# Second layer unrolled with a closer expert order; blank rows and expert weights placed in the first layer

## The reference

```python
x = x + ln(attention_16_heads(ln(x)) + ln(x))          # first layer, heads of 8 features, 256 tokens each
x = x + ln(ffn(ln(x)))                                 # second layer

def ffn(x):
    y = ln(x + mha(x)) * g1 + be1                      # 4 heads of 32, attention over the 16 sequences
    logits = y @ Wg.T                                  # 8 experts
    e = argmax(logits)                                 # one expert for each of the 4,096 tokens
    moe = relu(y @ W1[e] + b1[e]) @ W2[e] + b2[e]      # 128 -> 512 -> 128
    return ln(y + moe) * g2 + be2
```

## Time and profile before

| what | value |
|---|---|
| median of 3 runs | 700.91 us (698.33 to 701.24) |
| the profiled execution, its own time | 701.92 us |
| its span, first to last instruction | 700.2 us |
| TensorE's mean granted clock | 0.922 |
| busy share PE, DVE, ACT, POOL | 83%, 61%, 54%, 44% |
| first layer | 0 to about 376.5 us |
| second attention with the sort | about 376.5 to 574 us |
| experts | about 575 to 700 us |

### The profile page before, as it was taken

One profiled execution on the slowest core, in us unless ns is written; L12 is line 12 of the kernel. 1 busy time (PEld: TensorE's weight loads), 2 busy tenths in 40 slices (PEclk: granted clock), 3 DMA queues, 4 the chain that ended last, 5 costly groups with the idle time before them and its releaser, 6 DMA issues. The chain is left out here.

```text
span 700.2 us, 16679 instructions
## 1 busy us (share of the span) xinstructions
PE 581.0 (83%) x5511; PEld 432.2 (62%) x5511; DVE 428.4 (61%) x1210; ACT 377.7 (54%) x991; POOL 305.5 (44%) x535
## 2 busy tenths in 40 slices
PE   4999999999999999999972888888878109999920
PEld 3655666666666666666641787777765109999910
DVE  2454666666666666666523578888885603788870
ACT  1014665565666655655560698878851004677760
POOL 5321133233332332322134537777767720077676
PEclk9999999999999999999995799999978558999975
DMA  5000000000000000000015500000001112144333
GB/s 152 13 2 2 4 1 18 17 7 13 17 18 17 18 18 18 7 12 18 17 33 169 140 2 1 1 2 0 0 22 43 56 57 66 34 59 61 34 32 32
DMA packets 28593, 21.60 MB, mean 31 GB/s; under 512 B 3514, under 2 KB 26850, under 8 KB 28515
## 3 DMA queue, kind: packets, MB, share of 16 engines
q1 hardware_dynamic: 21186, 15.29, 8.7%
q0 software_dynamic: 6640, 4.92, 5.1%
q10 hardware_dynamic: 688, 0.39, 0.2%
HBM read 10.11 MB, written 8.12 MB: 26 GB/s over the span
## 5 line engine op out<-in xcount | busy, mean ns | idle before, releaser
L383 DVE TENSOR_REDUCE nmax<-psA 128x2 f32<-128x512 f32 x256 | 165.1, 687 | 121.5 <-PE psA L206 121.2
L511 ACT ACTIVATE pr<-psB 128x512 f32<-128x512 f32 x250 | 135.8, 595 | 123.4 <-PE psB L223 122.7
L206 PE MATMUL psA<-km,q 24*128 24x256 f32 x768 | 139.8, 428 | 3.4 <-POOL km L606 2.1
L223 PE MATMUL psB<-q,km 26*128 26x256 f32 (+1 forms) x752 | 109.9, 411 | 0.0
L206 PEld LDWEIGHTS psA<-km,q 24*128 24x128 f32 x768 | 91.7, 198 | 29.3 <-issue 17.5
L1620 POOL DMA_INDIRECT out<-wz,ys x39 | 61.1, 1568 | 60.7 <-ACT wz L1585 54.3
L606 POOL TENSOR_TENSOR km<-kraw,rows_of 128x768 f32<-128x768 f32 x16 | 23.5, 1467 | 118.6 <-DVEq L362 114.6
L237 PE MATMUL psO<-pr,v 128*32 128x256 f32 x1024 | 69.4, 389 | 1.3 <-ACT osb L505 1.1
L223 PEld LDWEIGHTS psB<-q,km 26*128 26x128 f32 (+1 forms) x752 | 69.0, 189 | 0.2 <-issue 0.2
L580 POOL TENSOR_SCALAR ve<-mv_r 128x2 f32<-128x2 f32 x16 | 3.7, 232 | 123.5 <-DVE mv_r L344 123.5
L1489 DVE TENSOR_TENSOR hT<-psH,e_nb1T 128x512 f32<-128x512 f32 x39 | 27.0, 692 | 42.4 <-PE psH L1450 33.0
(11 more groups left out here) (203 smaller groups left out, 1224.0 us busy)
## 6 DMA issues: line engine op xcount, KB each, us to landing
ys<-y_sorted SPq DMA_DIRECT2D x39, 72.0 KB, 1.8
xs<-x_all SPq DMA_DIRECT2D x16, 128.0 KB
e_w<-W SPq DMA_DIRECT2D x1, 2048.0 KB
e_w<-W SPq DMA_DIRECT2D x4, 512.0 KB
out<-x_all SPq DMA_DIRECT2D x15, 128.0 KB, 3.7
x_all<-x SPq DMA_DIRECT2D x1, 1536.0 KB, 10.0
q<-mT SPq DMA_DIRECT2D x64, 4.0 KB
out<-wz,ys POOLq DMA_INDIRECT x39
```

The source lines that it names most:

```text
L206: last = T.matmul(psA[:, n % 2, c * L1:(c + 1) * L1], queries(b, h, depth, slice(c * P, (c + 1) * P)), keys(b, h, depth, slice(0, L1)), st ...
L223: last = T.matmul(bank_of(b, h)[:, c * L1:(c + 1) * L1], keys(b, h, depth, slice(c * P, (c + 1) * P)), queries(b, h, depth, slice(0, L1)), ...
L383: V.tensor_reduce(nmax[:, b % 2, :, h], psA[:, n % 2, :].rearrange("p (c m) -> p c m", c=2), AX.X, ALU.max, negate=True).then_inc(S["a_fre ...
L511: A.activation(pr[:, h % PRING, :, :].rearrange("p c l -> p (c l)"), bank_of(b, h), ACT.Exp, scale=SCALE1).then_inc(S["b_free"], 1)
```

## The change

Weights and blank rows: the nine loads of expert parameters move from SP at the start of the second block to ScalarE's queue in iterations 1 to 5 of the first layer, two per iteration. GpSimd makes the blank rows in iteration 1 of the first layer, and ScalarE writes them over the whole region of each expert, one region at the start of each of the iterations 6 to 13, and over the region of the spare blocks in iteration 14. SP's fills after the sort are gone, as is the cast of the row numbers for them. `send` waits for the nine fills.

```diff
+            def fill(e):
+                act.wait_ge(S["blank_ok"], 1)
+                lo, hi = e * REGION, (e + 1) * REGION if e < NE else LAST_ROW
+                rows = blank[:, e:e + 1, :].broadcast_to([P, NT + 1, YROW]) if e < NE else blank[:, NE:, :]
+                act.dma_start(y_sorted[lo:hi, :].rearrange("(m p) d -> p m d", p=P), rows).then_inc(blanked, 16)
...
             for i in range(LAST + 3):
+                if 1 <= i <= 5:
+                    for to, source in loads[2 * i - 2:2 * i]:
+                        act.dma_start(to, source, allow_slow_non_contiguous=True).then_inc(loaded, 16)
+                if 6 <= i <= 6 + NE:
+                    fill(i - 6)
                 iteration(i)
...
-            for to, source in loads:
-                sp.dma_start(to, source, allow_slow_non_contiguous=True).then_inc(loaded, 16)
...
-            for e in range(NE):
-                r = sp.value_load(pad_i[0:1, e:e + 1], min_val=0, max_val=LAST_ROW - P)
-                sp.dma_start(y_sorted[bass.ds(r, P), :], zeros[:, e, :]).then_inc(S["padded"], 16)
```

```diff
-SORT_AT = {16: 0, 17: 1, 20: 2}
-BIAS_AT = 19
-SEND_AT = {17: (0, 0), 18: (0, 4), 19: (1, 0), 20: (1, 4), 21: (2, 0), 22: (2, 4)}
+CHUNKS = ((0, 8), (8, 8), (16, 8), (24, 4), (28, 4))
+SORT_AT = {12: 0, 16: 1, 20: 2, 22: 3}
+SEND_AT = {13: (0, 0, 2), 14: (0, 2, 2), 15: (0, 4, 2), 16: (0, 6, 2), 17: (1, 0, 2), 18: (1, 2, 2), 19: (1, 4, 2),
+           20: (1, 6, 2), 21: (2, 0, 2), 22: (2, 2, 6), 23: (3, 0, 4)}
...
+            def late_scales(i, n):
+                dve.wait_ge(S["yln_step"], 3 * i)
+                dve.wait_ge(S["sd_ok"], i - SETS + 1)
+                V.reciprocal(rs_y[:, :], sd_y[:, :]).then_inc(S["late_step"], 1)
+                dve.wait_ge(S["late_step"], i - SETS + 1)
+                V.scalar_tensor_tensor(out=nb_y[:, :], in0=mv_y[:, n, :, 0], scalar=-1.0, in1=rs_y[:, :],
+                                       op0=ALU.mult, op1=ALU.mult).then_inc(S["yln_step"], 1)
...
+            def late_norm(i, n):
+                act.wait_ge(S["yagg"], i + 1)
+                act.wait_ge(S["consts"], 2)
+                act.wait_ge(S["late_step"], i - SETS)
+                A.activation(sd_y[:, :], mv_y[:, n, :, 1], ACT.Sqrt, bias=eps[:, :]).then_inc(S["sd_ok"], 1)
+                act.wait_ge(S["yln_step"], 3 * i + 1)
+                for c in range(2):
+                    last = A.activation(yn[:, c, :], r2[:, n, c, :], ACT.Identity, bias=nb_y[:, c:c + 1],
+                                        scale=rs_y[:, c:c + 1])
+                last.then_inc(S["yln_step"], 1)
```

```diff
+                if (g := at(t, 4)) is not None:
+                    first_norm(g)
+                if (g := at(t, 9)) is not None:
+                    second_norm(g, range(0, min(2, SIZES[g])))
+                if (g := at(t, 10)) is not None:
+                    second_norm(g, range(2, SIZES[g]))
...
-            for t in range(STEPS):
-                for g, k in members(t, 11):
-                    put(FIRST[g] + k)
+            for t in range(NS):
+                put(t)
```

More of the change, by code:

```diff
@@ L29, in count, with first_layer @@
     return max(value, 0) if isinstance(value, int) else value
-def first_layer(nc, x, w_qkv, b_qkv, w_o, b_o, ident, identh, minus_half, xs, out, kept, loads2, loaded2):
+def first_layer(nc, x, w_qkv, b_qkv, w_o, b_o, ident, identh, minus_half, xs, out, kept, loads2, loaded2, loads,
+                loaded, blank, y_sorted, blanked):
     with ExitStack() as ctx:
@@ L644, in _ @@
                 iteration(i)
+                if i == 1:
+                    blank_rows()
         @block.sync
@@ L813, in pipeline, with run @@
         def pipeline(iteration):
[L816 to L822, removed]
+            def run():
+                for t in range(NSTEP + 8):
                     iteration(t, t % 4)
@@ L826, in late, with rooted @@
         def late(t):
-            return isinstance(t, int) and t >= NSTEP
+            return t >= NSTEP
+        def rooted(t):
+            return t >= NSTEP + 2
         block = ctx.enter_context(nc.Block())
@@ L903, in iteration @@
                     pe.wait_ge(S["lg_ok"], count(t - 8))
+                    pe.wait_ge(S["sums_read"], sum(at < t for at in SORT_AT))
+                    if t in SORT_AT:
+                        sums(SORT_AT[t])
                     if has(t, 4):
@@ L1016, in find @@
             def find(k):
-                n = SORT_STEPS * k + 4
+                first, n = CHUNKS[k]
                 dve.wait_ge(S["sums_full"], k + 1)
-                V.tensor_copy(run[0][:, Z:, :].rearrange("p j e -> p (j e)"),
-                              psQK[:, CHUNK * NE:2 * CHUNK * NE]).then_inc(S["sorting"], 1)
-                dve.wait_ge(S["sorting"], n + 1)
-                for step in range(3):
+                sort_step(V.tensor_copy(run[0][:, Z:Z + n, :].rearrange("p j e -> p (j e)"),
+                                        psAL[:, SUMS + n * NE:SUMS + 2 * n * NE]))
@@ L1024, in find @@
+                steps = n.bit_length() - 1
+                for step in range(steps):
                     a, b = run[step % 2], run[1 - step % 2]
-                    V.tensor_tensor(b[:, Z:, :], a[:, Z:, :], a[:, Z - 2 ** step:Z + CHUNK - 2 ** step, :],
-                                    ALU.add).then_inc(S["sorting"], 1)
-                    dve.wait_ge(S["sorting"], n + 2 + step)
-                V.tensor_tensor(place[:, :, :], psQK[:, 0:CHUNK * NE].rearrange("p (j e) -> p j e", e=NE),
-                                run[1][:, Z - 1:Z - 1 + CHUNK, :], ALU.add).then_inc(S["sorting"], 1)
@@ L1088, in iteration @@
                     V.tensor_copy(y_all[:, bass.ds(i * 2, 2), 0:P], yout[:, n, :, :]).then_inc(S["y_kept"], 1)
-                if late(t) and has(t, 6):
-                    finish_y(t - 6, m % 2, t)
+                if rooted(t) and has(t, 6):
+                    late_scales(t - 6, m % 2)
                 if has(t, 5):
@@ L1107, in iteration @@
                     last.then_inc(S["yagg"], 1)
+                if late(t) and has(t, 6):
+                    finish_y(t - 6, m % 2, t)
                 if has(t, 8):
@@ L1318, in iteration @@
                     last.then_inc(S["start_ok"], 1)
-                if has(t, 6):
+                if has(t, 6) and not rooted(t):
                     i, n = t - 6, m % 2
@@ L1423, in at @@
             return None
-        def members(t, lag):
-            turns = [(g, t - (ends(g) - 1 + lag)) for g in range(GROUPS)]
-            return [(g, k) for g, k in turns if 0 <= k < SIZES[g]]
-        STEPS = NS + 14
+        STEPS = NS + 11
         block = ctx.enter_context(nc.Block())
```

248 lines of the change are left out of this document (123 added, 125 removed).

## The result

The changed kernel took a median of 702.59 us (699.62 to 706.53 in undisturbed executions), the kernel before 701.17 in as many executions beside it: a ratio of 1.0036, with a 95% interval of 1.0019 to 1.0054. The loss of 0.36% is clear of zero by its interval, but it is less than the 0.5% that was named ahead of time as the bound of a change. Forecast were 690.1, a gain, and a range of 679 to 701. The profiled execution took 701.88 us and spans 700.1, so its parts can be set directly against the 700.2 of the profile before.

The account below looks back on a forecast made before the run. TensorE was taken to bound the first layer and the expert tiles, with waits for GpSimd, SyncE's blank-row stores and outstanding adds elsewhere. Terms -0.8 + 3.6 + 4.5 + 4.1 - 7.0 - 11.4 - 3.8 = -10.8 gave 690.1 us, range 679 to 701.

Parts of the forecast that it names:

- The fills in the first layer: First layer: weight loads and blank-row fills issued by ScalarE cost nothing; SyncE's small loads beside them bounded at 0 to 1 us per iteration.
- The rival that a fill's issue holds ScalarE: First layer: each of eight large fills blocks ScalarE 3.6 to 7.9 us, 30.8 us in all, total 720.9; chance 0.13.
- The closing stretch: From last logits to first expert load: 13.8 us against 25.2, ended last by the bias product; -11.4 us.
- 64 products 8.9: After the last logits: TensorE's 64 products of the expert biases take 8.9 us.
- GpSimd's last 16 stores ... end about the same time: After the last logits: GpSimd's stores from the end of step 20 finish about when the bias product does.
- The bias product at the low clock: Rival, after the last logits: product begun at 1.2 GHz takes up to twice 8.9 us; total 698, chance 0.05.
- Steps 16 to 23: Late second layer: normalisation in steps 18 to 21 on ScalarE and VectorE removes 9.9 us of waits for GpSimd; net -7.0 us.
- Sorting and stores in steps 12 to 15: Second layer: sorting adds 3.6 us at step 12; two indirect stores per step add 4.5 us in steps 14 and 15.
- TensorE's clock: Second layer: a late step opens a gap that drops TensorE's clock for one step; +4.1 us, bounds 0 and four steps.
- The rival of a fall in every sorting step: Second layer: each of steps 13 to 16 runs at 1.2 GHz, 16.4 us; total 697.9, chance 0.17.
- The loop unrolled: Second layer: the first step of the loop's second pass loses its extra time; -0.8 us.
- The experts: Expert part: two fewer indirect adds outstanding when TensorE stops, at 1.89 us each; -3.8 us, bounds 0 and -5.7.

Follow-up runs that it names:

- the later fills: Changed kernel with each of the nine fills issued some 7 us into its iteration instead of at its start; median 694.87 us, ratio 0.9944 to the kernel before.
- the paced kernel: Changed kernel with the later fills, GpSimd issuing a store only when the store two places before has landed; median 691.36 us, ratio 0.9869 to the kernel before.
- the kernel before with pacing: Kernel before the change, GpSimd issuing a store only when the store two places before has landed; median 698.3 us, ratio 0.9962.
- that part alone: Kernel before the change with only its expert part replaced by that of the changed kernel; median 696.74 us, ratio 0.9963.

## Why the prediction was wrong

- **The fills in the first layer: 0 forecast, +4.8 measured (+6.4 with the low stretch).** The step that failed is "SyncE's small loads of row maxima share the DMA engines with a fill; nothing in the trace prices that, and I bound it at 0 to 1 us per iteration and take 0". The bound was nearly right (0.3 to 1.2 in each iteration, 0.6 in the mean), the choice within it wrong. The price of the data was right: 308 GB/s and 7.9 us forecast, 306 and 7.9 measured. What was put at nothing is the load beside it: it has 4.6 us from issue to use, and beside a fill its first packet alone takes 3.4 us, where it took 1.15 before, and TensorE has it after 6.2. The rival that a fill's issue holds ScalarE was wrong too: 0.38 us.
- **The Trainium skill** (DMA: Bandwidth & Descriptors, Queues, rings and completion order) says that each DMA engine takes turns between the queues that have work, a packet at a time. By that rule SyncE's 4 KB would pass beside a fill. In this case 6.2 us went by between its issue at 194.99 and TensorE's start at 201.17, 3.4 of them before its first packet, and the measurement decides. Once a transfer has started the trace agrees: with the later fills SyncE's 128 KB move beside a fill from 199.63 to 202.84.
- **The closing stretch: -11.4 forecast, -2.6 measured.** What ends it, and when the product begins, came out as the sum had them. The failed term is "64 products 8.9": 17.5, and 8.88 when no store runs beside it. No rival had this. A second size was wrong and is hidden by the first: "GpSimd's last 16 stores ... end about the same time" leaves out what follows the last of them, 4.0 us to the first expert load in the paced kernel. By that the stores alone would have ended the stretch of the changed kernel at 570.47 + 4.0, after 16.6 us instead of 13.8 (an estimate from these two profiles); the paced kernel, whose stores come later, has 19.26. "The bias product at the low clock" priced up to twice 8.9, for another reason: the parts that ran took 6.2 and 4.6 us, in good part at the low level, but the 7 us of gaps between them are the hold.
- **Steps 16 to 23: -7.0 forecast, -3.6 measured, -6.9 with pacing** (49.36 to 42.42). The wait that the term removes did go, from the 9.9 us of the earlier trace rows to

```profile
DVE yg L1075 <- ACT yn L1221: 0.9, 1, 0.9
```

What the term left out is that a GpSimd freed of the normalisation works off eight stores in a row, which holds ScalarE in step 18 for 3 us. The change removed one wait for GpSimd and made another. That the paced kernel comes out at the very number of the forecast does not prove the price: the stage also lost the bias product and took on other sorts and stores, and no run has the normalisation alone.
- **Sorting and stores in steps 12 to 15: right.** Sorting was put at +3.6; steps 12 and 13 are 1.4 and 2.4 longer than the 8.26 of those ahead, 3.8. Two stores per step were put at +4.5 for steps 14 and 15; taking them away gave back 1.8 and 2.2.
- **TensorE's clock: +4.1 forecast, nothing measured.** The step that failed is that a step at the low level is longer by its products. There is one stretch at the low level (485.5 to 492, clock 0.50), mostly in step 13. The paced kernel has two (471.2 to 478.0 and 491.7 to 498.5), its stage reads 0.84 instead of 0.92, and the four steps take 41.74 us instead of 41.75. The rival of a fall in every sorting step is out. The Trainium skill (TensorE: Matmul & The Clock Gate, HAM oscillation — how this bites in real kernels) would have each round start cold; the trace shows it once in four steps, and twice in the paced kernel.
- **The loop unrolled: -0.8 forecast, about -1.0 up to step 11 and the loop's return at step 12 besides.** Of the -2.5 in the table, 1.5 lie in one step near the start (6.39 us between ScalarE's copies of `xy` against 7.83; 7.87 in the paced kernel, and 4.93 in the kernel before with pacing), and so aren't the unrolling's.
- **The experts: -3.8 forecast, -4.4 to -5.1 in the profiles**, 1.4 to 3.9 by the timing of that part alone. The size is nearly right, half of it for another reason. Twelve adds start behind TensorE's end, as forecast; but the same count gives 13 before, since the first of the 14 in the earlier trace rows starts at 670.47 and TensorE ends at 670.51. So one add fewer is outstanding and not two, and the tail behind TensorE's end falls by 2.0 us (29.7 to 27.6). The rest is TensorE's own stretch from its first to its last product, 93.2 before and 90.3 after, for which the sum had no term; with the old order it took 91.9 in another execution, so how much of it is the order's stays open.

The sum of the terms, -10.8, is close to what the kernel gives when both holes are closed: 691.36 against the forecast 690.1, and -11.5 in the profile. That is in part luck. By stage, the closing stretch gains 5.6 us less than forecast, and this is made good by steps 12 to 15, which cost 4.1 less because the clock's term did not come, and by 1.7 up to step 11 that no term had. The first layer's loss and the loss in the closing stretch are two meetings that the sum did not have: a small load with a fill, and the other engines' instructions with a row of stores.

## What to carry to other kernels

A transfer moved off the end of a kernel is not free because its issue is: ask which small transfer with a deadline is issued while it moves, and put it behind that one. A step in which GpSimd stays free of arithmetic can be filled with queued indirect stores, but here a long row of them cost the other engines; a wait in GpSimd's queue for the landing of the store two places before took most of that cost away. Where two candidates for the end of a stretch are nearly equal, removing one buys almost nothing, so price both, with what follows each, before moving either.

## What the hardware showed that was not expected

While GpSimd works off a row of queued indirect stores, the instructions of other engines at times come 0.70 us or a multiple apart: TensorE's products (seven instructions between 567.49 and 573.16), VectorE's table, ScalarE's copy in step 18, SyncE's stores in the kernel before (15.3 to 16.4 us for eight, 9.1 with pacing). It sets in some 8 to 17 us after the row begins, not for every engine at once, and it ends 1.4 to 2.7 us after the last store. It is not the clock, not the code's place and not the drain, as the runs show. That it needs a long row follows from the paced kernels, which send the same stores with a shorter queue and three pauses in the last row. How long a row it takes was not tried. For ScalarE in step 18 the trace shows a semaphore increment that arrives 2.95 and 9.4 us after the product that raises it; why it comes late, and what the others wait for (the profile says "issue"), stays open.

Beside a 2.4 MB fill, a transfer of another queue starts late: 3.4 us from issue to the first packet for SyncE's 4 KB loads instead of 1.15, 3.7 for its 128 KB store, and then it moves beside the fill. What holds it ahead of the DMA engines is open.
